# Attention scores as three products of split operands, keys split by GpSimd, with a new opening, a 16-column router and the first routing placed earlier

## What is computed

```
x = x + mamba(layernorm(x))
# cross-attention, 16 heads of 16 columns, 64 context rows per sequence
q = layernorm(x) @ Wq + bq;  k = ctx @ Wk + bk;  v = ctx @ Wv + bv
scores = q_h @ k_h.T, masked where s > l;  attn = softmax(scores / 4)
x = x + (attn @ v) @ Wo + bo
# mixture of experts: one shared, 8 routed, the best two of each row
h = layernorm(x);  logits = h @ Wr;  p, i = top_k(softmax(logits), 2)
x = x + shared(h) + sum over the two of p / sum(p) * expert_i(h)
```

## Time and profile before

| | us |
|---|---|
| median of 3 runs (lowest, highest) | 924.18 (923.59, 925.94) |
| the profiled execution | 925.91 |
| its span, first to last instruction | 924.3 |
| PE busy in the span | 892.2 (97%) |
| DVE busy | 624.8 (68%) |
| ACT busy | 524.0 (57%) |
| POOL busy | 329.1 (36%) |

### The profile page before, as it was taken

One profiled execution on the slowest core, in us unless ns is written; L12 is line 12 of the kernel. 1 busy time (PEld: TensorE's weight loads), 2 busy tenths in 40 slices (PEclk: granted clock), 3 DMA queues, 4 the chain that ended last, 5 costly groups with the idle time before them and its releaser, 6 DMA issues.

```text
span 924.3 us, 20525 instructions
## 1 busy us (share of the span) xinstructions
PE 892.2 (97%) x6798; PEld 781.0 (85%) x6799; DVE 624.8 (68%) x1464; ACT 524.0 (57%) x1050; POOL 329.1 (36%) x318
## 2 busy tenths in 40 slices
PE   6999998999998999999999999999999999999996
PEld 4688996566555878898888899999999999999996
DVE  4989796899977866665656657575565657575553
ACT  3694433656455554446454767575676757575552
POOL 3467222311302455454555133223232322322222
PEclk9999999999999999999999999999999999999999
DMA  8400020000002021112126555335353533533332
GB/s 223 145 1 1 1 84 9 1 2 1 1 8 93 26 72 61 61 71 73 50 83 208 167 139 138 47 47 138 47 138 47 138 47 47 138 47 47 47 47 35
DMA packets 87839, 64.00 MB, mean 69 GB/s; under 512 B 58096, under 2 KB 80816, under 8 KB 87664
## 3 DMA queue, kind: packets, MB, share of 16 engines
q0 software_dynamic: 17504, 34.87, 16.5%
q1 hardware_dynamic: 60624, 26.87, 11.3%
q10 hardware_dynamic: 9664, 1.62, 1.0%
HBM read 38.58 MB, written 24.77 MB: 69 GB/s over the span
## 4 chain that ended last, share of the span: by engine, by line
PE 77%; DVE 9%; issue 5%; ACT 3%; DMA 3%; POOL 2%; SPq 1%; DVEq 0%; ACTq 0%; POOLq 0%
PE PS L137 22%; PE PS L139 21%; PE PS L138 21%; PE PS L878 3%; PE PS L307 2%; DMA metar<-routed_rows 2%; PE PS L908 2%; PE PS L922 1%; PE PS L928 1%; DVE mxpad L1122 1%; ACT hideh L1897 1%; DVE hidl L143 1%; POOL routed_rows L1563 1%; PE PS L288 1%; ACT act32e L1899 1%
## 5 line engine op out<-in xcount | busy, mean ns | idle before, releaser
L1928 POOL DMA_INDIRECT out_rows<-y,toki x70 | 113.3, 1619 | 266.4 <-DVE y L1958 247.7
L1897 ACT ACTIVATE hideh<-PS,be 128x256 fp32r<-128x256 f32 x280 | 142.9, 510 | 101.8 <-PE PS L139 86.9
L143 DVE TENSOR_TENSOR hidel<-act32e,hideh 128x256 fp32r<-128x256 f32 x280 | 118.1, 425 | 83.7 <-ACT act32e L1899 79.8
L137 PE MATMUL PS<-xTeh,wfch 128*128 128x256 f32 x560 | 158.7, 283 | 2.0 <-ACT act32e L1899 1.1
L137 PE MATMUL PS<-wprh,hideh 128*128 128x256 f32 x560 | 158.6, 283 | 0.3
L139 PE MATMUL PS<-xTeh,wfcl 128*128 128x256 f32 x560 | 157.7, 282 | 0.0
L138 PE MATMUL PS<-xTel,wfch 128*128 128x256 f32 x560 | 157.7, 282 | 0.0
L139 PE MATMUL PS<-wprh,hidel 128*128 128x256 f32 x560 | 156.5, 279 | 0.0
L138 PE MATMUL PS<-wprl,hideh 128*128 128x256 f32 x560 | 156.3, 279 | 0.0
L1899 ACT ACTIVATE act32e<-PS,be 128x256 f32<-128x256 f32 x280 | 143.8, 514 | 7.5 <-DVE hidel L143 6.9
L137 PEld LDWEIGHTS PS<-xTeh,wfch 128*128 128x128 f32 x560 | 105.4, 188 | 3.6 <-issue 1.6
(11 more groups left out here) (271 smaller groups left out, 2072.2 us busy)
## 6 DMA issues: line engine op xcount, KB each, us to landing
xb<-routed_rows SPq DMA_DIRECT2D x144, 64.0 KB
fcraw<-in_Wfc POOLq DMA_DIRECT2D x8, 1024.0 KB
prraw<-in_Wproj POOLq DMA_DIRECT2D x8, 1024.0 KB
X<-in_x SPq DMA_DIRECT2D x8, 512.0 KB, 7.6
out_rows<-X SPq DMA_DIRECT2D x8, 512.0 KB, 2.9
routed_rows<-pads SPq DMA_DIRECT2D x8, 272.0 KB
out_rows<-y,toki POOLq DMA_INDIRECT x70
ctx<-in_ctxT SPq DMA_DIRECT2D x4, 256.0 KB, 7.0
```

Of the source, the lines that this page charges most:

```text
L137: nc.tensor.matmul(out, wh, xh, start=first, stop=False)
L143: return eng.tensor_tensor(out, whole, high.bitcast(F32), ALU.subtract)
L1897: nc.scalar.activation(hid[0][:, j, :], PS[:, j % 4, 0:BLK], ACT.Gelu_apprx_tanh, bias=bias)
L1928: nc.gpsimd.indirect_dma_start(out=out, out_offset=bass.IndirectOffsetOnAxis(ap=toki[:, h:h + 1], axis=0), in_=y[:, h, :], in_offset=None, ...
```

## The change

**Scores.** Queries and keys are split. ACT's `evac_q` writes the high part `qTh`; a new DVE instruction `q_low(b, m)` (PSUM + bias - high, 128x512) writes `qTl` and only it releases the scores (`qT_ready`). POOL's new `split_keys(b)` makes the two parts `kpair` of one sequence's keys (a cast and a subtraction, 128x512 each) into two places used in turn, so it waits for `key_scores(b-2, 1)`. Each score matmul becomes three, of fp32r. The subtraction for the shared expert's weights moves from DVE to POOL (`weight_low`).

**Opening.** PE first runs 16 matmuls of `ones` x `ones`, float32, 128x128, whose result is not used. `ones` is written before `onesrow`. The first 512 rows arrive as two loads. Four of the six small loads are issued by ACT instead of SP. DVE normalises the first rows before it waits for `w_in`.

**Router.** High and low columns of `wr` lie side by side (16 columns), so `logits` is four matmuls (it also adds the low x low term), and `choose` adds the two halves when it reads them. `ranks` is five matmuls, of 40, 32, 24, 16 and 8 columns, into bank 4.

**First routing.** For sequence 0, `transpose_logits` runs right behind `key_scores(7, 1)`, and `ranks` ahead of `up(0)`; `choose(0)` on DVE moves ahead of the residual and of `stats_part(1)`, `invert_sums(7)` ahead of `stats_part(1)`, and `place_rows`, `place_slots` and `place_gates` of sequence 0 ahead of `att_residual(7)` and the first `lows`. ACT copies the logits ahead of the last `exps` and runs `gates(0)` ahead of all `gelus(0)`. POOL sends the rows of sequence 0 before `add_bias(1)`.

The core of the diff:

```diff
+            WARM = 16
-                x_load(0)
+                for h, sem in enumerate((x_in[0], x0_rest)):
+                    sp.dma_start(X[:, 2 * h:2 * h + 2, :],
+                                 d["x"][0, 2 * h * P:2 * (h + 1) * P].rearrange("(t p) d -> p t d", p=P)).then_inc(sem, 16)
...
+                pe.wait_ge(ones_ready, 1)
+                for _ in range(WARM):
+                    nc.tensor.matmul(PS[:, 5, 0:P], ones[:], ones[:], start=True, stop=True)
                 pe.wait_ge(w_in, W_IN)
-                pe.wait_ge(ones_ready, 1)
...
+            PARTS = ((0, 0), (0, 1), (1, 0))
...
                     pe.wait_ge(qT_ready, KD * b + KD)
+                    pe.wait_ge(k_split, b + 1)
...
                     for m in range(KD):
-                        for half in range(2):
...
+                        for n, (qp, kp) in enumerate(PARTS):
+                            for half in range(2):
...
                                 last = nc.tensor.matmul(
-                                at, qT[rows, b % 2, m, t * P:(t + 1) * P],
-                                kbd[rows, b, m, :].rearrange("p (i n) -> p i n", i=2),
+                                    at, qT[qp][rows, b % 2, m, t * P:(t + 1) * P],
+                                    kpair[b % 2][kp][rows, m, :].rearrange("p (i n) -> p i n", i=2),
...
-                    for j in range(NG):
-                        rows = slice(32 * j, 32 * j + 32)
-                        nc.tensor.matmul(PS[:, j, :], kbd[rows, b, m, j % 2 * P:(j % 2 + 1) * P],
-                                         qT[rows, b % 2, m, :], start=True, stop=False, skip_group_check=True)
+                    for n, (qp, kp) in enumerate(PARTS):
+                        for j in range(NG):
+                            rows = slice(32 * j, 32 * j + 32)
+                            nc.tensor.matmul(PS[:, j, :], kpair[b % 2][kp][rows, m, j % 2 * P:(j % 2 + 1) * P],
+                                             qT[qp][rows, b % 2, m, :], start=n == 0, stop=False,
+                                             skip_group_check=True)
...
+                def split_keys(b):
+                    if b >= 2:
+                        pool_wait(pool, s_psum, 2 * NG * (b - 1))
+                    kh, kl = kpair[b % 2]
+                    nc.gpsimd.tensor_copy(kh[:], kbd[:, b]).then_inc(k_high, 1)
+                    pool_wait(pool, k_high, b + 1)
+                    low(nc.gpsimd, kl[:], kbd[:, b], kh[:]).then_inc(k_split, 1)
...
                 pool_wait(pool, bo_ready, 1)
+                for b in range(2):
+                    split_keys(b)
                 add_bo(0)
                 for b in range(1, B):
                     if b + 1 < B:
                         rstds(b + 1)
+                        split_keys(b + 1)
                     add_bo(b)
+                    if b < 5:
+                        weight_low(b - 1)
...
+                def q_low(b, m):
+                    dve.wait_ge(q_high, KD * b + m + 1)
+                    nc.vector.scalar_tensor_tensor(qT[1][:, b % 2, m, :], PS[:, q_bank(b, m), :], bq[:, m:m + 1],
+                                                   qT[0][:, b % 2, m, :].bitcast(F32), ALU.add,
+                                                   ALU.subtract).then_inc(qT_ready, 1)
...
                 def second_stats():
                     stats_part(1)
+                    for m in range(KD):
+                        q_low(0, m)
...
+                    if after:
+                        q_low(b + 2, 0)
                     divide(b)
+                    if after:
+                        q_low(b + 2, 1)
...
-                    for k in range(KD):
-                        last = product(PS[0:E, 4, :], [w[:, k, :] for w in wrp],
-                                       [x[:, k, :] for x in xTs[b % 2]], k == 0, k == KD - 1)
+                    for i, x in enumerate(xTs[b % 2]):
+                        for k in range(KD):
+                            last = nc.tensor.matmul(PS[0:2 * E, 4, :], both_wr[:, k, :], x[:, k, :],
+                                                    start=i + k == 0, stop=i + k == KD)
```

139 lines of the change are left out of this document (80 added, 59 removed).

## The result

The changed kernel takes 921.05 us (median of 20 runs, 917.85 to 924.46) beside 924.96 us for the kernel before on the same chip (20 runs, 921.56 to 928.17). The ratio is 0.9958, 95% interval 0.9946 to 0.9969: 3.9 us faster, between 2.9 and 5.0. The forecast was 4.6 faster, in the range of 910.5 to 924.5.

What follows compares the result with a forecast made beforehand. PE was taken to bound the kernel, except attention rounds, set by a chain through DVE. Opening -2.5, attention +3.3, way into the shared expert -0.8 and router -4.6 sum to -4.6: 924.18 to 919.6 us, range 910.5 to 924.5.

Steps and rivals of the forecast that it cites:

- opening: Start of the kernel: warming matmuls and earlier loads start the z projection earlier; -2.5 us, between -0.5 and -4.2.
- scores, attention: Attention: entry +3.8 and rounds -0.5 together cost +3.3 us, between +1.5 and +5.5.
- way into the shared expert: First sequence's routing moved earlier, between attention and shared expert: -0.8 us, between 0 and -2.5.
- router: Router in the other seven sequences: fewer `logits` and `ranks` matmuls, 7 x 0.66 = -4.6 us, between -3.9 and -4.8.
- Rival B: Opening: clock falls before the z projection, warming buys only the start; opening -0.5, time 921.6 us; chance 0.17.
- Matmuls: Score matmuls on PE: `row_scores` from 1.07 to 0.90 to 0.95 us, `key_scores` 0.15 to 0.20 shorter, weight loads hidden.
- D: Score matmuls: twelve or sixteen weight loads queue, making a score step weight bound; 922 to 930 us; chance 0.03.
- The step that the round stands on: Attention round: two `q_low` lengthen DVE's fourth-to-first `maxima` stretch from 8.15 to 9.1 us; round 19.5 against 19.26.
- Entry: Entry to attention: `q_low` delays `residual(5)` and `out_part(6)`, POOL's splits may slow `hn`; +3.8 us, ends 3.2 and 4.8.
- C: Attention rounds: POOL's block slides into DVE's `divide`, `hn` and `o_low`; +6.6 us, time 930.8; chance 0.07.
- The price of one sequence: Router: `logits` saves 0.46 and `ranks` 0.2, so 0.66 us for each of seven sequences.

Runs made afterwards that it cites:

- the kernel with `hn` moved under that block: Changed kernel with reordered attention entry and rounds, plus half of `hn`, second residual and `x_low` moved later on DVE: 922.66 us, ratio 0.9974.
- a new entry and half of `hn` moved: Changed kernel with `q_low(0, .)` behind `residual(5)`, POOL's first splits before `rstds(1)`, second half of `hn` directly behind first `maxima`: 917.06 us, ratio 0.9900.
- both orders: Changed kernel with `q_low(0, .)` behind `residual(5)`, earlier POOL splits, first `maxima` before `o_low`, and `project_o`'s first piece behind second `key_scores`: 915.93 us, ratio 0.9903.

## Why the prediction was right or wrong

The difference was forecast 0.7 us too large, but that is a sum of larger misses: the scores cost 2.3 more, the opening gave 0.6 and the move 1.2 more than taken. The scores' cost lies just above the end of its own range, and the router's gain alone below its. That the sum came so near is partly luck.

| term | predicted | measured |
|---|---|---|
| opening | -2.5 (-0.5 to -4.2) | -3.1 (alone) |
| scores, attention | +3.3 (+1.5 to +5.5) | +5.6 (left out), +5.7 (alone) |
| way into the shared expert | -0.8 (0 to -2.5) | -2.0 (left out) |
| router | -4.6 | -1.7 alone; both -6.5 (0.9897 to 0.9967) |

- **Opening.** Rival B's condition came, its price did not: z starts 2.2 earlier, by small matmuls and transposes at the high clock as forecast, and then the clock does fall in most traces, around 11 us. For this case the prediction kept 0.5 to 1.5, B 0.5. Measured are 3.1, and 3.0 in the trace of after: the start of z gives 2.2, and z itself 0.7, though the clock falls in it (6.97 for 7.71). Right was that what is won stays, and that the warming gives it: without it nothing is won.
- **Matmuls.** `row_scores` takes 0.92 (196.50 - 195.58), in the forecast's 0.90 to 0.95, and the twelve weight loads cost nothing seen. That is D's end. The Trainium skill (TensorE: Matmul & The Clock Gate, section LDWEIGHTS) gives a load of 32 rows and one of 128 rows the same time. The traces agree, with 0.18 and 0.19 us; a queue of such loads, of which the page says nothing, is what the earlier trace rows contradicts, with eight in 0.31. `key_scores(., 0)` came down to 1.36 as forecast, but `key_scores(., 1)` from 1.53 to 1.48 only.
- **Round.** The step that the round stands on held: 9.04 for DVE (forecast 9.1), then 1.36, 0.92. Between the second `key_scores` and `weigh_values` it says 1.36 + 2.13 = 3.49; it is 3.68, and PE is busy all of it, since that `key_scores` is 0.12 longer than I had it (1.48 for 1.36) and PE, no longer ACT, ends it. So 19.62 instead of 19.5, +0.36 instead of +0.2 in rounds 2 to 4. That PE idles 1 to 1.5 ahead of the second `row_scores` is right, though most of it stands ahead of the piece of `project_o`, for `o_low`. By the offsets: round 0 -1.0 (forecast -0.9), round 1 +0.8 (+0.6), rounds 2 to 5 together +1.05 (+0.8), round 6 -0.6 (-1.0). Sum +0.2 instead of -0.5.
- **Entry.** -3.00 to +1.20 in after's offsets, 4.2 against 3.8 taken and 4.8 as the end. `out_part(6)` waits 2.25 (forecast 2.4) for the reason given; `hn` takes 3.60 beside POOL; `key_scores(0, 0)` waits 1.65 instead of 0.9, as forecast.
- **The mis-sized term is therefore the sum of attention:** 4.4 in the traces for 3.3 (0.7 in the rounds, 0.4 at the entry), and 5.6 in the medians. The last 1.2 are open. In the traces of the changed kernel with and without its scores 1.1 of them lie in the routed loop (407.2 and 406.1), which the change doesn't touch. The clock could take part: the granted clock, a mean over the timed runs, is 0.991 in the changed kernel beside 0.993 without its scores, and (0.9933 - 0.9908) x 919 us is 2.3 us of full clock lost. But none of the nine traces with the new scores has a fall in the rounds, up to 268 us, where PE idles about 1 us a round.
- **C** didn't come: POOL's block takes 0.61 + 1.28 + 2.8 + 2.38, less than the 2.1 + 2.8 + 2.8 of the sum; it begins at 198.12 and ends at 205.3, and the next `divide` of DVE is at 209.0 (189.34 + 19.62). But its mechanism is real: the kernel with `hn` moved under that block lost 6.6 us.
- **First routing.** The step that failed is a sentence: "POOL's earlier `send_rows(0)` moves nothing that PE waits for." I followed the engines' lists and not the buffer: ACT's next copy into `rows` waits for POOL's stores, and DVE and PE wait behind ACT. Without the move PE waits 2.02 us there, with it not at all. In the trace of before PE runs at the low clock at 329 to 332 and comes too late to wait; the opening alone shows the wait, 1.40. That the placing steps delay what follows was right (`up(0)` +0.85 later against the fourth `maxima`).
- **Router.** The price of one sequence was right (0.66; 0.69 measured). That all seven come by themselves was wrong: without the move one of them is lost to that same chain, and of the gain alone (1.7) another 2.5 are missing without a cause shown. Router and move together give 6.5, as 4.6 and 2.0 would.

**The best kernels** of this study are the changed one without its scores (0.9897), with a new entry and half of `hn` moved (0.9900), and with both orders (0.9903): equal within their intervals, all 5 to 6 us below the change as it is. The scores as three products pay for themselves only after DVE's order is mended, and then gain nothing over leaving them alone. The new orders with the old scores were not tried.

## What to carry to other kernels

Shorter matmuls bought with work on a second engine are worth what that engine's chain allows; add up the chain between two waits, as here 9.1 us, and not the busy shares, and see what now fills the gaps before moving it. Moving a step early can be worth more for the buffer that it frees than for the work: follow who overwrites what it wrote. And put a piece of the same program side by side in several traces before reading a difference of 1 to 2 us in one pair.
